# A two-layer attention and expert kernel: layer 1's routing cut into 37 parts in the last steps of the heads, and its row sends moved towards the last heads

## What is computed

```python
xn = _layernorm(x, axis=-1)
s = _L1_attn_ref(xn, ...)   # 16 heads of 128 in 4 groups; rope, alibi, 30*tanh(./30), causal softmax, @ Wo + bo
g = _silu(_L1_ffn_ref(xn, ...))
x = x + s * g

# in _L1_ffn_ref: 32 experts, 4 chosen for each row, and one shared
logits = flat @ router_w.T
scores = jnp.sqrt(jax.nn.softplus(logits))
_, idx = jax.lax.top_k(scores + expert_bias, K)
topv = jnp.take_along_axis(scores, idx, axis=1)
topv = topv / (topv.sum(axis=-1, keepdims=True) + 1e-20)
probs = jnp.zeros((T, E), flat.dtype).at[jnp.arange(T)[:, None], idx].set(topv)
# out = sum over experts of p * (silu(clip(x @ wg.T)) * clip(x @ wu.T)) @ wd.T, and the shared expert
```

## Time and profile before

| | |
|---|---|
| median of 3 runs | 857.31 us (856.62 to 862.87) |
| the profiled execution | 856.94 us, of which the span is 855.2 |
| PE busy | 783.4 us, 92% of the span |
| DVE busy | 611.4 us, 71% |
| ACT busy | 465.4 us, 54% |
| POOL busy | 423.7 us, 50% |
| layer 1's heads | 340.0 to 711 us of the span |
| MoE and the end | 711 to 855.2 us |

### The profile page before, as it was taken

One profiled execution on the slowest core, in us unless ns is written; L12 is line 12 of the kernel. 1 busy time (PEld: TensorE's weight loads), 2 busy tenths in 40 slices (PEclk: granted clock), 3 DMA queues, 4 the chain that ended last, 5 costly groups with the idle time before them and its releaser, 6 DMA issues.

```text
span 855.2 us, 13950 instructions
## 1 busy us (share of the span) xinstructions
PE 783.4 (92%) x4871; PEld 639.4 (75%) x4871; DVE 611.4 (71%) x1077; ACT 465.4 (54%) x822; POOL 423.7 (50%) x479
## 2 busy tenths in 40 slices
PE   6999999978777878898999999999999999999996
PEld 5776776754222367687988889989999999998884
DVE  8588868557998767888967886766767654445555
ACT  4433342279888733676645556565656555655431
POOL 1767837333555445445434447568663412665540
PEclk9999999998999989999999999999999999999999
DMA  5211194000000041000000001111110569643107
GB/s 182 75 38 37 38 292 135 1 1 1 1 1 1 1 126 30 22 7 11 21 8 13 8 25 57 38 38 49 47 44 1 207 126 351 214 149 106 51 5 243
DMA packets 50116, 59.82 MB, mean 70 GB/s; under 512 B 13559, under 2 KB 41084, under 8 KB 50048
## 3 DMA queue, kind: packets, MB, share of 16 engines
q1 hardware_dynamic: 45488, 50.49, 19.4%
q0 software_dynamic: 4560, 8.44, 2.8%
HBM read 41.11 MB, written 21.86 MB: 74 GB/s over the span
## 4 chain that ended last, share of the span: by engine, by line
PE 56%; DVE 12%; ACT 6%; POOL 6%; issue 5%; DMA 1%; POOLq 0%; ACTq 0%; DVEq 0%; SPq 0%
PE ps L786 12%; PE ps L516 8%; PE ps L518 8%; PE ps L517 8%; PE ps L879 4%; PE ps L876 3%; PE ps L910 3%; DVE cap L1477 2%; POOL A L1772 2%; DVE swap L1467 2%; PE ps L858 2%; PE ps L698 2%; PE ps L558 2%; PE ps L613 1%; PE ps L795 1%
## 5 line engine op out<-in xcount | busy, mean ns | idle before, releaser
L1131 ACT ACTIVATE cap<-cap 128x1024 f32<-128x1024 f32 (+7 forms) x128 | 87.1, 680 | 123.1 <-DVE cap L1477 123.0
L786 PE MATMUL ps<-V,P 128*128 128x129 f32 x1152 | 152.7, 279 | 0.0
L786 PEld LDWEIGHTS ps<-V,P 128*128 128x128 f32 x1152 | 145.3, 194 | 2.7
L1477 DVE SCALAR_TENSOR_TENSOR cap<-dist,ps 128x1024 f32<-128x1024 f32 (+7 forms) x128 | 95.1, 750 | 27.1 <-PE ps L518 22.1
L1696 POOL TENSOR_SCALAR_AFFINE_SELECT P<-P 128x128 f32<-128x128 f32 x128 | 38.8, 303 | 148.6 <-ACT P L1136 148.3
L1828 POOL DMA_INDIRECT y_scratch<-y_sb,aux_s x63 | 62.1, 985 | 61.2 <-ACT y_sb L1176 39.3
L1136 ACT ACTIVATE P<-cap 128x1024 f32<-128x1024 f32 (+7 forms) x128 | 87.6, 685 | 4.1
L516 PE MATMUL ps<-q_hi,k_hi 128*128 128x512 f32 x192 | 72.2, 376 | 7.9 <-DVE cap L1477 6.3
L518 PE MATMUL ps<-q_lo,k_hi 128*128 128x512 f32 x192 | 66.9, 349 | 0.0
L517 PE MATMUL ps<-q_hi,k_lo 128*128 128x512 f32 x192 | 66.8, 348 | 0.0
L1803 POOL TENSOR_TENSOR rot<-rot,swap 128x512 f32<-128x512 f32 x40 | 52.2, 1306 | 14.4 <-DVE swap L1467 14.2
(11 more groups left out here) (288 smaller groups left out, 2111.6 us busy)
## 6 DMA issues: line engine op xcount, KB each, us to landing
xg_scratch<-blank SPq DMA_DIRECT2D x1, 8127.0 KB, 31.2
xa<-xg_scratch SPq DMA_DIRECT2D x63, 128.0 KB, 2.3
ew<-in_experts SPq DMA_DIRECT2D x3, 1920.0 KB, 7.9
y<-y_scratch SPq DMA_DIRECT2D x8, 512.0 KB, 5.0
pk<-in_packed SPq DMA_DIRECT2D x8, 384.0 KB, 3.2
pks<-in_scales SPq DMA_DIRECT2D x8, 384.0 KB, 4.3
ew<-in_experts SPq DMA_DIRECT2D x1, 3072.0 KB, 11.2
wqk<-in_wqk SPq DMA_DIRECT2D x20, 128.0 KB, 2.0
```

Source lines behind the costliest of these rows:

```text
L786: last = pe.matmul(ps[:, 4 + r % 2, o:o + D1 + 1], P1[:, h % 2, a:a + P], V1[:, j, h // REP, :], start=(j == 0), stop=(j == t))
L1131: act.activation(cap[:, n % 2, 0:w], cap[:, n % 2, 0:w], ACT.Tanh, scale=1.0 / (CAP * float(D1) ** 0.5))\
L1477: dve.scalar_tensor_tensor(out=cap[:, n % 2, 0:w], in0=dist[:, 0:w], scalar=slope, in1=psf[:, 1024 * (n % 2):1024 * (n % 2) + w], op0=ALU. ...
```

## The change

The router's parts become 37 in place of 30: parts 1, 2, 3 and 13 of before are cut into shorter ones, with the same instructions in the same order. The numbers in `ROUTER` place them, but for part 0 and the four slot lists, behind steps 4 to 7 of heads 2 to 10; two parts may now share a step. The logarithm of ACT moves from step 10 to 14, the square root from 16 to 30, the ranks from head 4 to head 7. The 32 sends stand from step 74 to 123 instead of from 57 to 100, none behind steps 0 and 1 but two in head 15.

```diff
--- before.py
+++ after.py
@@ -1515,36 +1515,40 @@
                     link(dve.tensor_scalar(r_a[:], r_c[:], 1.0, None, ALU.is_equal))
                 elif part == 1:
                     dve.wait_ge(sp_a, 2)
-
                     link(dve.tensor_scalar(r_c[:], r_c[:], -1.0, None, ALU.add))
                     link(dve.tensor_tensor(r_c[:], r_c[:], r_a[:], ALU.add))
+                elif part == 2:
                     link(dve.tensor_tensor(r_d[:], r_d[:], r_a[:], ALU.add))
+                elif part == 3:
                     link(dve.reciprocal(r_a[:], r_c[:]))
+                elif part == 4:
                     link(dve.tensor_tensor(r_d[:], r_d[:], r_b[:], ALU.mult))
-                elif part == 2:
                     link(dve.tensor_tensor(r_d[:], r_d[:], r_a[:], ALU.mult))
+                elif part == 5:
                     link(dve.tensor_scalar(r_c[:], lg[:], 0.0, None, ALU.max))
                     dve.tensor_tensor(r_a[:], r_d[:], r_c[:], ALU.add).then_inc(sp_b, 1)
-                elif part == 3:
+                elif part == 6:
                     dve.wait_ge(sp_b, 2)
                     dve.wait_ge(sp_a, 3)
-
                     link(dve.tensor_scalar(r_c[:], r_b[:], 1e-30, None, ALU.max))
+                elif part == 7:
                     link(dve.reciprocal(r_d[:], r_c[:]))
+                elif part == 8:
                     link(dve.tensor_tensor(r_d[:], r_d[:], r_a[:], ALU.mult))
                     link(dve.tensor_tensor(r_d[:], r_d[:], r_b[:], ALU.add))
+                elif part == 9:
                     link(dve.tensor_scalar(r_b[:], r_d[:], 0.5, None, ALU.mult))
                     eb = ebias[:].rearrange("p (t e) -> p t e", t=1).to_broadcast((P, NT, NE))
                     link(dve.tensor_tensor(r_a[:], r_b[:], eb, ALU.add))
-                elif part < 8:
-
-                    for t in (2 * (part - 4), 2 * (part - 4) + 1):
+                elif part < TOP_PARTS + 4:
+
+                    for t in (2 * (part - TOP_PARTS), 2 * (part - TOP_PARTS) + 1):
                         link(dve.max(top[:, t, :], r_a[:, t, :]))
                         link(dve.max_index(topi[:, t, :], top[:, t, :], r_a[:, t, :]))
-                elif part == 8:
+                elif part == TOP_PARTS + 4:
                     link(dve.tensor_copy(topf[:], topi[:]))
-                elif part < 9 + TOPK:
-                    k = part - 9
+                elif part < TOP_PARTS + 5 + TOPK:
+                    k = part - TOP_PARTS - 5
                     dst = r_m if k == 0 else r_c
                     link(dve.tensor_tensor(dst[:], each_tile(iota[:]), topf[:, :, k:k + 1].to_broadcast((P, NT, NE)),
                                            ALU.is_equal))
@@ -1554,14 +1558,15 @@
                             ins.then_inc(rk_ready, 1)
                         else:
                             link(ins)
-                elif part == 13:
+                elif part == SUM_PARTS:
                     dve.wait_ge(rk_ready, 1)
                     link(dve.tensor_tensor(r_d[:], r_m[:], r_b[:], ALU.mult))
                     link(dve.tensor_reduce(r_sum[:], r_d[:], AX_X, ALU.add))
                     link(dve.tensor_scalar(r_sum[:], r_sum[:], 1e-20, None, ALU.add))
+                elif part == SUM_PARTS + 1:
                     link(dve.reciprocal(r_inv[:], r_sum[:]))
                     link(dve.tensor_tensor(r_d[:], r_d[:], r_inv[:].to_broadcast((P, NT, NE)), ALU.mult))
-                elif part == 14:
+                elif part == SUM_PARTS + 2:
 
                     whole = [r_b[:, i, :].bitcast(I32) for i in range(2)]
                     dve.wait_ge(rk_read, 1)
@@ -1569,26 +1574,26 @@
                     link(dve.tensor_scalar(whole[1], whole[0], 7, None, ALU.arith_shift_right))
                     link(dve.tensor_copy(r_t[:, 1, :], whole[1]))
                     link(dve.tensor_tensor_scan(r_t[:, 2, :], r_t[:, 1, :], r_t[:, 1, :], 0.0, ALU.add, ALU.max))
-                elif part == 15:
+                elif part == SUM_PARTS + 3:
 
                     link(dve.tensor_tensor(r_t[:, 4, :], r_t[:, 2, :], r_t[:, 1, :], ALU.subtract))
                     link(dve.tensor_tensor(r_t[:, 4, :], r_t[:, 4, :], iota[:], ALU.subtract))
                     link(dve.tensor_scalar(r_t[:, 5, :], r_t[:, 4, :], float(P), float((NE - 1) * P), ALU.mult, ALU.add))
                     link(dve.tensor_scalar(r_t[:, 6, :], iota[:], float(P), None, ALU.mult))
-                elif part == 16:
+                elif part == SUM_PARTS + 4:
 
                     link(dve.scalar_tensor_tensor(out=r_c[:], in0=r_k[:], scalar=float(P), in1=each_tile(r_t[:, 5, :]),
                                                   op0=ALU.is_ge, op1=ALU.mult))
                     link(dve.tensor_tensor(r_s[:], r_k[:], r_c[:], ALU.add))
-                elif part == 17:
+                elif part == SUM_PARTS + 5:
 
                     link(dve.tensor_tensor(r_s[:], r_s[:], each_tile(r_t[:, 6, :]), ALU.add))
                     link(dve.tensor_scalar(r_t[:, 3, :], r_t[:, 2, :], dist[:, 0:1], None, ALU.is_le))
                     link(dve.tensor_reduce(over_of, r_t[:, 3, :], AX_X, ALU.add))
                     link(dve.tensor_scalar(e_off[:], over_of, float(NE - 1), float(3 * D), ALU.min, ALU.mult))
-                elif part < 18 + 2 * TOPK:
-                    k = (part - 18) // 2
-                    if part % 2 == 0:
+                elif part < PICK_PARTS + 2 * TOPK:
+                    k = (part - PICK_PARTS) // 2
+                    if (part - PICK_PARTS) % 2 == 0:
                         link(dve.tensor_tensor(lg[:], each_tile(iota[:]), topf[:, :, k:k + 1].to_broadcast((P, NT, NE)),
                                                ALU.is_equal))
                         one = scr[:, 0:1, :].rearrange("p i (t e) -> p i t e", t=NT).to_broadcast((P, 2, NT, NE))
@@ -1596,7 +1601,7 @@
                     else:
                         link(dve.tensor_reduce(place_of[:, k], picked, AX_X, ALU.add))
                 else:
-                    k = part - 18 - 2 * TOPK
+                    k = part - PICK_PARTS - 2 * TOPK
                     if k >= 1:
                         dve.wait_ge(x_sent, 16 * NT * k)
                     link(dve.tensor_copy(slot_row[:, k, :], place_of[:, k, 0, :]))
@@ -1838,10 +1843,17 @@
 
 VAR_STEP = 2 * NT + 1
 
-ROUTER = {"act": [6, 10, 16], "dve": [8, 12, 14, 18, 20, 22, 24, 26, 27, 28, 29, 30, 31, 33] + [38 + 2 * i for i in range(4)]
-          + [46 + i for i in range(2 * TOPK)] + [55 + 12 * k for k in range(TOPK)]}
-RANKS_AT = 4
-SEND_AT = [57 + 12 * k + t for k in range(TOPK) for t in range(NT)]
+TOP_PARTS = 10
+SUM_PARTS = TOP_PARTS + 5 + TOPK
+PICK_PARTS = SUM_PARTS + 6
+ROUTER = {"act": [6, 14, 30],
+          "dve": [8, 20, 21, 22, 23, 28, 36, 38, 39, 44]
+          + [45, 46, 46, 47, 52, 52, 53, 54, 55]
+          + [60, 61, 62, 63, 68, 69]
+          + [70, 71, 76, 77, 78, 79, 84, 85]
+          + [72, 86, 101, 114]}
+RANKS_AT = 7
+SEND_AT = [*range(74, 80), 82, 83] + [87, *range(90, 96), 98] + [102, 103, *range(106, 112)] + [*range(116, 124)]
 MOE_EARLY = 3
 
 PROJ = [("k", 0)] + [p for h in range(H1) for p in ([("q", h)] + [("k", h // REP + 1)] * (h % REP == 2 and h // REP + 1 < G1))]
@@ -1906,8 +1918,8 @@
             later = []
         if name == "scores":
             out.append(s)
-            if engine in ROUTER and NT * s[1] + s[2] in ROUTER[engine]:
-                out.append(("router", ROUTER[engine].index(NT * s[1] + s[2])))
+            if engine in ROUTER:
+                out += [("router", part) for part, at in enumerate(ROUTER[engine]) if at == NT * s[1] + s[2]]
             if engine == "pool" and NT * s[1] + s[2] in SEND_AT:
                 out.append(("send", SEND_AT.index(NT * s[1] + s[2])))
         elif name == "context":
```

## The result

| | before | changed |
|---|---|---|
| median of 7 runs each, same chip (us) | 857.78 | 852.75 |
| lowest to highest (us) | 856.62 to 862.87 | 851.36 to 855.58 |
| span of the profiled execution (us) | 855.2 | 850.9 |

The ratio is 0.9931, with a 95% interval of 0.9911 to 0.9951: the changed kernel is 5.0 us faster. The forecast was 13.2 us. The measured 852.75 lies 1.3 us above the upper end of the range (851.5), and by the prediction's own line of 1% it counts as the same.

The account below looks back on a forecast made before the run. PE bounds each head, and time above the undisturbed lengths is waits caused by other engines. Removing 18.1 us and adding 4.9 gains 13.2: 856.94 to 843.7, as a median 844.1, stated as 844 us; range 838.5 to 851.5.

Parts of the forecast that it names:

- the paragraph on the end of the heads: SP's loads behind the later last send: aux_s keeps 5 us of cover, weights come some 5 us later, cost 0.
- the 3.4: Head 1's gain as parts 1 and 2 leave: 1.9 us of idle PE plus 1.5 for the lower clock.
- 19.1 + 5.1 + 1.1: Head 7: undisturbed 19.1 us, about 5.1 for the ranks moved there, 1.1 for part 19 before the turned context.
- the mechanism named: Head 6 start: parts behind step 5.4 delay DVE's output-projection sum, so PE waits 2.0 us for its bank.
- the 0.8 for head 8 to 9: Parts 23 to 26 and 33 fill DVE, so it enters head 9 some 0.8 us late: 0.8 added.
- the 0.5: End of head 9: parts 28 to 30, about 2.5 us, ahead of the last projection's sum, add 0.5 us.
- A: Rival: nothing new waits, DVE's slack in late steps covers all; 18.1 us gained, 839; chance 0.13.
- B: Rival: late steps fuller, parts stretched by POOL, lower clock behind two waits; 12.8 us lost, 852; chance 0.14.
- C: Rival: aux_s late, sharing engines with three weight groups issued behind it; 8 us gained, 849; chance 0.10.
- D: Rival: parts ahead of score biases stop PE in seven heads, 5.8 us each; slower, 880; chance 0.05.
- The added 4.9: New waits from parts in late steps of heads: 2.0 + 0.5 + 1.1 + 0.8 + 0.5 us.
- the 3.5: The added cost in us if parts in steps 5 to 7 cost their short form, by the exclusive port lock rule.

Follow-up runs that it names:

- group 5 later: Changed kernel with the last group of expert weights issued behind the load of row block 19 instead of 11: 848.5 us, 0.9868 of the kernel before.
- sends early: Changed kernel with the last two slot lists at steps 97 and 108, the last send at 116 instead of 123: 849.07 us, 0.9877 of before.
- late sends in the kernel before: Kernel before, router parts in place, but slot lists and sends at the changed kernel's positions: 862.22 us, 1.0032 of before.
- the second execution: The changed kernel itself, nothing altered, measured again: 851.55 us, 0.9940 of the kernel before.
- clearing the end of head 5: Changed kernel with parts 12 and 13 moved to step 6.4 and parts 14, 16 and 17 one step later: 849.48 us, 0.9903 of before.
- parts four steps earlier: Changed kernel with parts 1 to 18 each four steps earlier, same cut and sends: 856.85 us, 0.9998 of the kernel before.
- the kernel with three changes: Changed kernel with the last weight group later, sends packed earlier and clear of early head 9, parts placed with slack: 842.73 us, 0.9824 of before.

## Why the prediction was wrong

**Which step failed.** It is the paragraph on the end of the heads: "The weights come some 5 us later, and the first of them is wanted only by the tenth block. Cost 0." The dates in it were good. Shifted by the 14.2 us by which the MoE starts earlier, its rows "from 695 to 701", aux_s "at 702" and weights "at 703" were 694.8 to 700.0, 700.1 and 700.6. The cover of `aux_s` held too: it landed 6.6 us after its issue, and ACT never waits for it. The weights are not late either: PE never waits for them. But their bytes come 7 us later relative to the MoE (3 by their issue, 4 by the small packets ahead of them), and the question asked of them was only who wants the weights. Nobody asked what is issued behind them on the same queue: the rows of block 12, with a cover that the late weights used up. The term is not 0 but about 6 us: 4.2 to 4.4 of wait, 1.5 to 2.6 of slow blocks. The runs show it from both sides: group 5 later and sends early each remove the wait, late sends in the kernel before make it. The ratios put it at 4 to 6 us, each with 2 to 4 us of doubt. With 6 the sum would have been 13.2 - 6 = 7.2, or 850.6 from this comparison's 857.78. The 2 us that are still missing are of the size by which single executions differ in head 1 (0.9) and in the MoE's small waits (2.6); they stay open.

**The heads, term by term.** The sum came out (12.7 for 13.2), but by terms that missed on both sides:
- Head 1: 20.6, forecast 20.7. Partly luck: in the second execution it is 21.5. The lower clock behind head 0's wait of 2.0 us, which the change leaves alone, is longer or shorter from one execution to the next. Of the 3.4 only the 1.9 of idle PE is sure: the kernel before with late sends has head 1 at 21.3 with parts 1 and 2 still in it, since no lower clock came that time, so the 1.5 for the clock is a matter of the execution.
- Head 2: 21.2, forecast 20.1. PE still waits for two score biases, 0.58 and 0.44, so the gain was overrated by 1.1.
- Head 3: 19.7, forecast 19.1. Part 4 in step 2.7 reaches into it; moved, it is 19.1.
- Heads 4 and 7: 23.3 as forecast, and 24.9 against 19.1 + 5.1 + 1.1 = 25.3. If the 1.48 us of wait behind part 19 (forecast 1.1) is taken off, the ranks cost 4.3, not 5.1.
- Head 5: 21.2, forecast 20.8; one bias is 0.5 late.
- Head 6: 26.8, forecast 27.0, and by the mechanism named: 1.69 of wait for `s_tok`, removed by clearing the end of head 5.
- Heads 8 to 10: the 0.8 for head 8 to 9 did not appear (23.3 and 22.0); head 9 keeps 1.25 of wait where 1.0 was forecast, through the sends, as named, though a part beside the rotation would have done nearly the same (0.99). Head 10 has 0.4 of the 0.5.

**The rivals.** A needed no new waits; there are several. B gave 852, next to the measured time, but that is luck: the added waits came to 5.7 (below), not 12.8, none of them in heads 1 to 10 has the lower clock behind it, and the missing time is in the MoE. The lengthening that it names does occur (3.26 us for a part in head 9, below), but DVE had the room. C gave 849 and named the right place, SP's queue at the end of the heads, but the wrong victim: `aux_s` is not late, it makes others late. D did not happen: the longest new wait is 1.69 and the kernel is faster. It also counted seven heads with parts where there are nine, since head 3 has part 5 and head 10 two picks. Even parts four steps earlier, with waits of up to 2.20, only bring the gain to 0.

**The port rule.** The prediction took the lengthened part 16 (1.24 us) between two values, with the rule of the Trainium skill (SBUF — State Buffer, SBUF: two separate sides) as the lower one. The three rows from the kernel with three changes agree with the rule: L1600 arrives at 547.06 in a copy of POOL's that ends at about 547.6 and takes 1.11 instead of 0.69; the rotation arrives at 547.58 in L1600 and takes 1.73 instead of 1.27. Each second one is longer by 0.42 to 0.46, a little less than what was left of the first (0.57 and 0.59). But a part can be held for more than one operation. In the changed kernel part 27 meets three of POOL's in a row (timelines of DVE and POOL; the two others are the rows at 548.65 and 550.59 above):

```profile
548.90 3.26 DVE L1597 TENSOR_TENSOR scr<-iota,topf 128x256 f32<-128x256 f32 x1
549.91 0.73 POOL L1781 TENSOR_TENSOR wqk_lo<-wqk,wqk_hi 128x256 fp32r<-128x256 f32 x1
```

It takes 3.26 us where its kind takes 0.42, and ends 0.3 after the last of the three (3.24 in the second execution). The longest such operation in the prediction's rows took 1.44. Nothing on PE comes of it: DVE is through at 552.88 and then waits 0.23 for ACT. The added 4.9 came out as 1.7 + 1.5 + 0.4 + 0.6 (head 3) + 0.5 (head 5) + 1.0 (head 2), 5.7, and no wait of PE in it is shown to be the port's: it was neither 4.9 nor the 3.5 that the rule would have given, since the terms in heads 2, 3 and 5 were not in the sum at all.

## What to carry to other kernels

When a transfer is moved in time, go down the queue behind it to the end, and for each later transfer write when it is issued, what bytes stand ahead of it, and when its consumer wants it. A cover worked out for the moved transfer alone says nothing of the ones behind. And moving small work into a late step is free only up to the slack of what must be freed at the step's end; that slack can be read in the trace (here 1.8 us of parts cost nothing, and 4.2 cost a wait of 1.69), and a second cause of the same length may wait behind the one that is removed.

## What the hardware showed that was not expected

- A transfer of 63.0 KB in 8-byte pieces kept all 16 engines full for most of the 4 us from 688 to 692, at 38 GB/s. In the kernel before the same one is hidden, since nothing is issued behind it for 19 us.
- A DVE operation that met three POOL operations in a row was held through all of them: 3.26 us instead of 0.42, in a place where nothing waited for it.
- Waits of about 2 us of PE are followed by half speed sometimes: 2.50 us at 395.66 was (0.65 over the next 3.4 us), 2.20 at 461.21 was (0.65), 4.41 at 721.18 was (0.60 in the window around it), while the kernel before shows none behind 1.84. Behind the wait of 1.9 us at the same place of head 1 it read 0.65 in the kernel before and 1.00 in the kernel before with late sends. Behind the same wait of 2.0 us in head 0 the first step of head 1 took 4.7 us in some executions, 5.5 in others, and 3.1 in one.
